# Attention scores two heads at a time: a rewritten program of 128 steps, with the maxima's pair ahead of the exponentials' pair from the 15th step on

## What is computed

```python
qkv = (x @ Wqkv.T + bqkv).reshape(Bb, Ss, 3, H, HD).transpose(2, 0, 3, 1, 4)
attn = softmax(einsum('bhid,bhjd->bhij', q, k) / sqrt(HD), axis=-1)
comb = concatenate([x, cs_exp], axis=-1)
coh = sigmoid(tanh(comb @ Wc1.T + bc1) @ Wc2.T + bc2).transpose(0, 2, 1)
mod = attn * coh[..., None]
mod = mod / (mod.sum(-1, keepdims=True) + 1e-08)
fa = softmax(einsum('be,se->bs', fp, pe), axis=-1)     # one row per batch
mod = (1.0 - fi) * mod + fi * fa[:, None, :, None]
out = einsum('bhij,bhjd->bhid', mod, v).transpose(0, 2, 1, 3).reshape(Bb, Ss, Ee)
x = x + out @ Wout.T + bout
x = x + hamilton(q_left_n, hamilton(x * spectral_gate, conj(q_right_n)))
```

## Time and profile before

| what | value |
|---|---|
| median of 3 runs | 379.8 us (374.76 to 381.87) |
| span of the profiled execution | 375.9 us |
| its own time | not given apart from the three; it includes the span, which lies 3.9 us (1.0%) below the median |
| PE busy | 321.0 us (85%), 1537 matmuls |
| DVE / ACT / POOL busy | 223.9 / 176.9 / 156.8 us |
| mean granted TensorE clock | 0.904 of full speed |

### The profile page before, as it was taken

The page is one execution under the profiler, slowest core; times in us unless marked ns, Lnnn a source line. Parts: engine busy times, 40 slices in busy tenths (PEclk is TensorE's granted clock), DMA queues, the critical chain, the costliest instruction groups (busy, mean ns, idle before and its releaser), DMA issues.

```text
span 375.9 us, 5338 instructions
## 1 busy us (share of the span) xinstructions
PE 321.0 (85%) x1537; PEld 189.0 (50%) x1537; DVE 223.9 (60%) x385; ACT 176.9 (47%) x323; POOL 156.8 (42%) x129
## 2 busy tenths in 40 slices
PE   0848849999799889999799689999799779999975
PEld 0634426555456456655456356655456346544423
DVE  3765943786568616687577407686577517775102
ACT  2101103765356625556456415565356525667750
POOL 9979950099991000299400000199500030296000
PEclk9986975999989958999899958999899969999996
DMA  8698498214953992216924991125943990200001
GB/s 245 247 125 99 146 127 123 83 58 99 125 59 112 126 163 51 75 66 127 124 30 145 149 118 36 62 78 112 118 51 122 124 146 1 84 1 2 1 1 57
DMA packets 16518, 35.87 MB, mean 95 GB/s; under 512 B 2724, under 2 KB 8228, under 8 KB 14456
## 3 DMA queue, kind: packets, MB, share of 16 engines
q1 hardware_dynamic: 14968, 34.47, 50.4%
q10 hardware_dynamic: 1536, 1.23, 1.2%
HBM read 25.07 MB, written 10.50 MB: 95 GB/s over the span
## 4 chain that ended last, share of the span: by engine, by line
PE 63%; DMA 24%; DVE 4%; ACT 3%; issue 3%; SPq 1%; ACTq 0%; DVEq 0%
PE smax_ps L996 14%; PE st_ps L1018 14%; PE o_ps L1030 13%; DMA stack<-max_rows 10%; DMA stack<-qk_scratch 10%; PE job_ps L894 9%; PE job_ps L929 3%; PE job_ps L970 3%; ACT probs L594 2%; DMA qk_scratch<-qk_lo 2%; PE job_ps L951 2%; DVE qk_lo L672 2%; PE smax_ps L982 2%; DMA w_raw<-wqkvT 1%; DVE maxima L746 1%
## 5 line engine op out<-in xcount | busy, mean ns | idle before, releaser
L746 DVE TENSOR_REDUCE maxima<-smax_ps 128x1 f32<-128x512 f32 x256 | 168.3, 686 | 113.6 <-PE smax_ps L996 113.0
L594 ACT ACTIVATE probs<-st_ps 128x512 f32<-128x512 f32 x247 | 142.6, 597 | 137.0 <-PE st_ps L1018 135.6
L996 PE MATMUL smax_ps<-stack 127*128 127x512 f32 x256 | 118.0, 464 | 13.8 <-DMA stack<-qk_scratch 11.9
L1018 PE MATMUL st_ps<-stack 128*128 128x512 f32 x247 | 107.7, 439 | 19.8 <-DMA stack<-max_rows 18.2
L996 PEld LDWEIGHTS smax_ps<-stack 127*128 127x128 f32 x256 | 52.0, 204 | 51.5 <-DVE maxima L746 24.4
L1030 PE MATMUL o_ps<-probs,vals 128*32 128x512 f32 x512 | 71.7, 634 | 1.0 <-ACT probs L594 0.9
L1018 PEld LDWEIGHTS st_ps<-stack 128*128 128x128 f32 x247 | 50.5, 205 | 39.6 <-DMA stack<-max_rows 19.8
L419 POOL TENSOR_TENSOR vals<-v_new,vals 128x256 f32<-128x256 f32 x16 | 10.0, 641 | 94.5 <-PE o_ps L1030 94.5
L401 POOL TENSOR_TENSOR x_lo<-x_raw,x_hi 128x1024 fp32r<-128x1024 f32 x3 | 7.2, 2388 | 65.7 <-ACT x_hi L550 65.7
L894 PE MATMUL job_ps<-x_hi,w_hi 128*128 128x512 f32 x48 | 22.0, 459 | 10.0 <-DVE w_lo L797 9.5
L519 POOL TENSOR_TENSOR prod<-amap,x_tok 128x1024 f32<-128x1024 f32 x12 | 28.6, 2383 | 0.9
(11 more groups left out here) (105 smaller groups left out, 305.5 us busy)
## 6 DMA issues: line engine op xcount, KB each, us to landing
stack<-qk_scratch SPq DMA_DIRECT2D x64, 256.0 KB, 9.7
qk_scratch<-qk_hi SPq DMA_DIRECT2D x16, 256.0 KB, 2.0
qk_scratch<-qk_lo SPq DMA_DIRECT2D x16, 256.0 KB, 2.0
x_tok<-x SPq DMA_DIRECT2D x4, 512.0 KB, 12.0
out<-y SPq DMA_DIRECT2D x8, 256.0 KB, 2.2
x_raw<-xT SPq DMA_DIRECT2D x3, 512.0 KB, 12.1
pe_tab<-fa_rows SPq DMA_DIRECT2D x4, 256.0 KB, 3.8
row<-rows SPq DMA_DIRECT2D x1, 936.0 KB, 7.6
```

What stands on the lines that cost most here:

```text
L594: nc.scalar.activation(probs[:, t % RING, :], st_bank(b, t)[:, :], ACT.Exp, scale=SCALE).then_inc(exp_done, 1)
L746: nc.vector.tensor_reduce(maxima[:, g % 2, n:n + 1], smax_ps[smax_bank(u)][:, :], AX_X, ALU.max).then_inc(smax_reduced, 1)
L996: nc.tensor.matmul(smax_ps[smax_bank(u)][:, :], stack[0:MAX_ROW, 0, h, i * P:(i + 1) * P], stack[0:MAX_ROW, 1, h, :], start=True, stop=Tru ...
L1018: nc.tensor.matmul(st_bank(b, t)[:, :], stack[:, 1, h, j * P:(j + 1) * P], stack[:, 0, h, :], start=True, stop=True).then_inc(st_filled, 1)
```

## The change

The program is written anew. What it does:

- Scores have three terms (`TERMS = 3`) of 16 rows and one row for ones and maxima, 49 partitions in all. Two heads share a step: one lies in partitions 0 to 48, the other in 64 to 112. `STEPS` is 128 in all (32 a batch), and each step has two matmuls for the maxima (over 48 partitions) and two for the exponentials (over 49), each of 512 columns, into neighbouring banks.
- The exponentials' pair has one pair of banks, `st_all`; `scores(s)` waits for the exponentials of s - 1. From step 117 on (`WIDE` = 116) a second pair is used by turns. `exponentials` is one instruction over 1024 columns. The maxima have three banks: pair u waits until the first tile of pair u - 1 is reduced. DVE still reduces 256 tiles of 128x512, one by one.
- Steps 0 to 9 issue the exponentials' pair, then two maxima pairs; from 10 on one maxima pair, 14 steps ahead; from step 14 on (the 15th) the maxima pair stands ahead of the exponentials' pair on PE.
- Jobs are no longer in thirds: a projection is six matmuls in one step. q0 and k0 of the next batch stand at steps 3 and 5 of a batch (7 and 9 in the first), q1, k1, v0, v1, coh0, coh1 at 17, 21, 23, 25, 29, 31. Coherence's second product has its operands turned round. Output tiles are four jobs instead of two.
- x_hi and x_lo are doubled, so are the outputs y; `probs` holds 6 pairs.
- In following batches ACT makes one copy `qk_f`, and GpSimd makes `qk_hi` and `qk_lo` from it; DVE takes no part. SP writes the high part twice and the low part once for each side, and reads a group with two DMAs (48 partitions each, 768 KB in all instead of 1 MB). Maxima are stored by SP, no longer by ACT, in places written out in its queue.
- Group 0 of the first batch goes round DRAM no longer: `direct` multiplies with weights that stand three times, ACT and DVE write `stack` at once. The maxima of its first pair of heads go in before those of the second.
- The map's coefficients are built from 4x4 products on 64 partitions and spread by two matmuls; GpSimd no longer blanks `stack`.
- The loop over batches is written out.

The core of the diff:

```diff
-STEPS = G * IT * HG
-GS = IT * HG
-LEAD = 26
-RING = 8
-TERMS = 4
+TERMS = 3
+MAX_ROW = TERMS * HD
+HALF = P // 2
+PER = G * IT * 2
+GS = IT * 2
+STEPS = B * PER
+RING = 6
...
+LEAD = 14
+AHEAD = IT
+def smax_at(s):
+    if s < LEAD - AHEAD:
+        return range(AHEAD + 2 * s, AHEAD + 2 * s + 2)
+    return range(s + LEAD, min(s + LEAD + 1, STEPS))
...
+JOB_STEP = {"q0": 3 - PER, "k0": 5 - PER, "q1": 17 - PER, "k1": 21 - PER, "v0": 23 - PER, "v1": 25 - PER,
+            "coh0": 29 - PER, "coh1": 31 - PER, "max0": -5, "max1": 3, "max2": 11, "max3": 19, "z": 7, "zT": 9,
+            "field": 13, "tokens0": 11, "tokens1": 19, "tokens2": 27, "tokens3": PER + 1, "back0": 22,
+            "back1": PER + 2, "out0": PER + 7, "out1": PER + 9, "out2": PER + 13, "out3": PER + 15}
...
+            def scores_for_max(u):
...
+                wait(pe, smax_reduced, 2 * u + 2 - SMAX)
+                for a in range(2):
+                    at = a * HALF
+                    nc.tensor.matmul(smax_all[:, (2 * u + a) % SMAX], stack[at:at + MAX_ROW, 0, 2 * g + pp, i * P:(i + 1) * P],
+                                     stack[at:at + MAX_ROW, 1, 2 * g + pp, :],
+                                     start=True, stop=True).then_inc(smax_filled, 1)
+            def scores(s):
...
+                wait(pe, exp_done, st_before(s) + 1)
...
+                for a in range(2):
+                    at = a * HALF
+                    nc.tensor.matmul(banks[:, a], stack[at:at + MAX_ROW + 1, 1, 2 * g + pp, j * P:(j + 1) * P],
+                                     stack[at:at + MAX_ROW + 1, 0, 2 * g + pp, :],
+                                     start=True, stop=True).then_inc(st_filled, 1)
...
+            for s in range(STEPS):
+                if s < LEAD:
+                    scores(s)
+                for u in smax_at(s):
+                    scores_for_max(u)
+                if s >= LEAD:
+                    scores(s)
+                for n in range(B * G * IT):
+                    if av_step(n) == s:
+                        weigh_values(n)
+                jobs(s)
...
+            load_x(1)
+            for side in range(2):
+                write_hi(0, 0, side)
+                write_lo(0, 0, side)
+            read_stack(0, 1)
+            load_maxima(0, 0, 0)
```

More of the change, by code:

```diff
@@ L53 @@
[L53 to L57, removed]
-SMAX = 3
[L61 to L80, removed]
@@ L98 @@
[L98 to L116, removed]
@@ new lines, in job_steps @@
+def job_steps():
+    when = {}
+    for b in range(B):
+        for name, t in {**JOB_STEP, **JOB_STEP_OF.get(b, {})}.items():
+            if not (b == 0 and name == "max0") and not (b == B - 1 and name.startswith("out")):
+                when[name, b] = PER * b + t
+    return when
+JOB_AT = job_steps()
+JOB_ORDER = sorted(JOB_AT, key=lambda job: (JOB_AT[job], RANK.index(job[0])))
+LAST_OUT = STEPS - 9
+LAST_OUT_STEPS = {STEPS - 9: 0, STEPS - 7: 1, STEPS - 4: 2, STEPS - 3: 3}
+WIDE = STEPS - LEAD + 2
@@ new lines, in job_banks, with filled_before, st_pair @@
+def job_banks():
+    bank, before, last = {}, {}, {0: None, 1: None}
+    for n, job in enumerate(JOB_ORDER):
+        k = 0 if JOB_AT[job] >= LAST_OUT - 2 else n % 2
+        bank[job], before[job], last[k] = k, last[k], job
+    return bank, before, last[1]
+JOB_BANK, JOB_BEFORE, LAST_IN_1 = job_banks()
+def filled_before(job):
+    return sum(JOB_BANK[other] == JOB_BANK[job] for other in JOB_ORDER[:JOB_ORDER.index(job)])
+def st_pair(s):
+    return 1 if s >= WIDE and (s - WIDE) % 2 else 0
@@ L386, in _ @@
+            for half in range(2):
+                store(B - 1, half)
             sp.wait_ge(out_stored, 16 * 2 * B)
@@ new lines, in max_row, with coherence_hidden @@
+            def max_row(job, b, g):
+                ps = filled(act, job, b)
+                n = IT * 2 if job in ("maxA", "maxB") else 2 * GS
+                before = max_count(b, g) - 1 if job not in ("maxA", "maxB") else "AB".index(job[-1])
+                wait(act, max_loaded, 32 * before)
+                nc.scalar.activation(max_rows[0:n, :], ps[0:n, 0:P], ACT.Copy, scale=-1.0).then_inc(max_rows_done, 1)
+            def coherence_hidden(b, blk):
+                ps = filled(act, f"coh{blk}", b)
+                if b == 0:
+                    act.wait_ge(hE_done, 4)
+                nc.scalar.activation(hT[:, blk, :], ps[:, :], ACT.Tanh,
+                                     bias=percond[:, b, blk:blk + 1]).then_inc(h_ready, 1)
@@ L681, in values @@
+            def values(b, half):
+                ps = filled(dve, f"v{half}", b)
+                if half == 0:
+                    wait(dve, v_ready, G * b)
+                    wait(dve, v_sum_done, b)
+                if b == 0:
+                    dve.wait_ge(ld_row, 16)
                 nc.vector.tensor_tensor(
@@ new lines, in project, with direct @@
+                ins.then_inc(done, 1)
+            def direct(pp, side):
+                if side == 0:
+                    pe.wait_ge(ld_wdir[pp], 16)
+                ps = (st_all[:, side], job_ps[side][:, :])[pp]
+                c0 = (2 * pp + side) * P
+                for k in range(KT):
+                    ins = nc.tensor.matmul(ps, w_dir[:, k, c0:c0 + P], x_raw[:, k, :], start=(k == 0),
+                                           stop=(k == KT - 1))
+                ins.then_inc(dir_filled, 1)
```

1411 lines of the change are left out of this document (734 added, 677 removed).

## The result

The changed kernel takes 340.66 us, the median of four runs (338.68 to 344.77), against 380.84 for the kernel before beside it on the same chip (374.76 to 382.06). The ratio is 0.905, with a 95% interval of 0.893 to 0.917: faster by 40 us. I had forecast 300 with a range up to 333. The execution in the profile is the longest of the four (344.77 us, span 342.8; the others have spans of 336.7 to 338.8). My sum gave a span of 297, so 45.8 us of the profiled one have to be found; some 4 to 6 of them belong to this execution alone.

A forecast was written before the change was run, and what follows sets the result against it. The prediction took PE, busy 85%, as the bound, with DMA hand-overs between batches. Start 38, steps 0 to 9 with stalls to 72, steps 10 to 115 to 269, last steps to 284, end 297 of span: 300 us, range 280 to 333.

The forecast's parts named there:

- The floor: Shortest step, set by the round between PE and ACT through one pair of banks: 1.65 us.
- A: Rival: the two matmuls of a pair run one behind the other on PE; 2.16 us a step, 337 us; chance 0.12.
- C: Rival: PE falls to half clock from standing a little every step; 2.8 us a step, 406 us; chance 0.03.
- D: Rival: a queue place or bank claim on PE waits for another engine once a group; near 375 us; chance 0.02.
- B: Rival: the maxima pair ahead of the exponentials' pair holds PE up for DVE; 4 us a batch, 316 us; chance 0.15.
- The step, 1.86: Mean step of a batch of 59.4 us, taken for the 106 steps 10 to 115: 197 us.
- sign that PE would wait most for ACT: Sign of a right forecast: PE waits most for ACT's exponentials, no longer for DMAs between batches.
- Steps 0 to 9: Ten early steps with two maxima pairs each, set by DVE's four reductions, 2.5 us a step: 25 us before other work.
- 6 of field, bias and value work: DVE's other work in steps 0 to 9, 6 us added to 25 for reductions: 31 us.
- The start, 38: Time from the start of the span to the first exponentials' pair on PE: 38 us.
- Stalls, 3 (0 to 12): Waits in steps 0 to 9 from SP's queue and GpSimd's late values: 3 us, range 0 to 12.
- rival A: The same rival as A, pairs one behind the other on PE; its 333 us of span nearly sets the range's end.

The follow-up runs named there:

- e3_same_rows: Changed kernel with both matmuls of every pair reading partitions 0 to 48, so the second head gets the first's scores: 426.11 us, ratio 1.141 to the kernel before.
- e2_scores_first: Changed kernel with the exponentials' pair ahead of the maxima pair on PE in every step: 333.57 us, ratio 0.894 to the kernel before.
- e8_spread: Changed kernel with, in steps 0 to 9, one maxima pair ahead of the jobs and one behind: 331.29 us, ratio 0.890 to the kernel before.
- e6_all: Changed kernel with the edits of e1_field, e5_maxima_ahead and e8_spread together: 320.02 us, ratio 0.861 to the kernel before.
- e5_maxima_ahead: Changed kernel with SP issuing the first maxima's transfer ahead of k0's last write and group 1's read: 332.55 us, ratio 0.895 to the kernel before.
- e10_filled: e6_all plus unread matmuls on PE, 20 before the first scores and some around the jobs of the first steps: 319.45 us, ratio 0.846 to the kernel before.
- e1_field: Changed kernel; GpSimd does the field's power before the second batch's q and k, and output weights after DVE's pair sums: 335.73 us, ratio 0.894 to the kernel before.
- e7_warm: Changed kernel with 36 unread matmuls on PE while it waits for the first maxima: 337.53 us, ratio 0.910 to the kernel before.

## Why the prediction missed

**The floor and the pairs: right.** From the end of one exponentials' pair to the start of the next I had 0.6; it is 0.63 where PE did wait for ACT (97.60 + 1.02 to 99.25), which makes the floor 1.65 as forecast. The instruction over 1024 columns is 1.025, I took 1.05. Side by side, taken from the sets over quarter columns, is what half rows do, and `e3_same_rows` shows what A would have cost. A, C and D are refuted for the steady state, and B's price by `e2_scores_first`. The split of q and k by GpSimd was hidden there as forecast, and no `stack` wait stands in any batch. DVE's count of reductions stood.

**The step, 1.86: 0.05 short.** Of the long odd step (2.08; measured 2.25) the term for two pairs was 0.48 and no change between them; one pair is followed by the next after 0.34, not 0.24, though both use half rows. The projection is 1.58 with its change of mode, for 1.50. That is 4 us in 84 steps. The even steps, 1.67 for my 1.65 to 1.70, are right by luck: I had the floor as what sets them and PE's work at 1.54, with the set at 0.86 where 1.00 less 0.10 is 0.90. PE's work is 0.34 + 0.33 + 1.00, 1.67, and it sets them; it happens to equal the floor. So my sign that PE would wait most for ACT did not come: 1.9 us, against 22.6 for maxima.

**"Steps 0 to 9: four reductions, 2.5 us; this is DVE's, PE has 2.2": the step that failed.** The DVE sum was good, 31 us against 29.9 measured. It was not the bound. I took the longer of two sums, as if DVE's work and PE's overlapped freely. With three banks they don't: a step goes pair 0.34, pair 0.34, wait 0.82, pair 0.43, set 1.0 and jobs up to 1.6 one after the other, 4.5 us at full clock, and DVE stands during the last two. PE's own sum was too small besides, 22 us for the ten steps: PE was busy 41.7 us at a mean clock of 0.76, by an estimate 32 at full clock. The terms of the 2.2 I did not write down, so which of them is short can't be said. Of the 17 us, the order of `e8_spread` gives back 5 at the same clock (`e6_all`, 46.1 for 51.3). The clock gives back at least 2 (`e5_maxima_ahead`, 49.0 at 0.85, and `e10_filled`, 43.9 at 1.00 with unread matmuls in it, for 46.1). The rest no run removes; by the estimate above PE work that my sum didn't have may be all of it, which is not shown.

**"6 of field, bias and value work": mis-sized, and its order left out.** The field's chain has a link on GpSimd. I had priced GpSimd's load (34 us a batch, light) and not its queue: a 0.58 us operation behind the split cost DVE 2.85 us of waiting, and four operations of 2.3 us took 5.4. It made one step of 10.6 us in place of 1.9. The step alone fell by 7.2 us in `e1_field` (10.64 to 3.40), and the stretch 10-32 from 56.2 to 48.1, of the 15 us that it had over my sum. What the stretch should take is seen in the next batch, where the same 22 steps at full clock took 42.5 or 42.6 us in every profile with this order of the pairs and side by side. Over that, the changed kernel has 13.7: step 12 has 7.9 (10.64 for 2.75), step 17 1.8 (4.10 for 2.27), and steps 13, 14 and 18, at half clock, 3.3. In `e1_field` 5.6 are left, half of it in steps 13 and 14 at half clock. So the two places of the field's work are some two thirds of the excess, and the steps at half clock most of the rest. This is near to rival D, a place in a queue that waits for a job of another engine, which I had looked for only behind the first batch.

The Trainium skill (SBUF — State Buffer, "Who interferes with whom") has one pair of SBUF ports shared by the vector engine and GpSimd, held for a whole instruction. The trace agrees: DVE's operation at 98.39 of `e1_field` ended 0.28 us behind GpSimd's at 98.21, and the one of step 17 did so in nine profiles. By that rule such an operation is to be priced at what GpSimd has left to do, here up to 1.27 and 2.4 us, not at its own 0.3 to 0.8.

**"The start, 38": 6.6 short, 5 of it in the term ahead of the read.** The read and the maxima behind it took 7.4 us (36.38 to 43.77) for my 6.8. The read was issued at 36.4, by my terms it would have been 31. The first maxima pair was even early (14.31 for 16.2); behind it came the second `direct` (3.78 and 2.69 us), a wait of 2.96 for its low part, and q0 and k0, all on PE one behind the other and most of it at half clock (0.50 from 14.2 to 20.8 and from 24.5 to 31.1), which I had put "between" as if free. I had seen that the maxima stand behind the read in SP's queue, and priced it as given; `e5_maxima_ahead` shows that this place alone was worth about 8 us of the start.

**"Stalls, 3 (0 to 12)"** were a guess for queues. The range ended at 333 since I let rival A set it; no rival was about the first rounds. Three terms that failed in the same direction made 39 of the 45.8 us.

## What to carry to other kernels

Price a pipeline's first rounds on their own, by the chain through the engine that is claimed and the buffers between, not by the busiest engine's sum: with one or two buffers, what PE does between two claims is time in which the reader stands. When an engine looks idle by its load, walk its queue at each point where a small result of it is wanted; a half-microsecond operation behind others stopped three engines here, and putting it first took 5 us out of one step. Small operations of one engine beside long ones of another can each last as long as those. Small loads that free a waiting engine go ahead of large ones in the issuing queue.

## What was not expected of the hardware

The granted clock fell to the lower level, 1.2 GHz, with no long wait ahead: in `e7_warm` between 51.83 and 52.38, where PE's waits were of 0.91 us, once a step. In a kernel with longer matmul pairs (`e3_same_rows`) it fell in mid-run, though PE was almost always busy (63.98 of 65 us from 150 to 215). I have no rule for it from these runs.

Consecutive pairs over half rows are 0.34 apart where two matmuls over all rows are 0.23 apart: about 0.10 is paid between pairs of the same mode (0.57 in `e3_same_rows` is 0.23 twice and that 0.10, by an estimate).

A read of 384 KB into the two groups of rows landed in 5.4 us, median of 30, where one of four 256 KB reads had 9.7; two transfers carry a group where four did.
